# Matmuls of constants in TensorE's waits: a two-layer vision tower on one core

## The reference, cut to what matters

```
x: (32, 3, 96, 96) -> tok: 16x16 patches and four shifted copies, projected, layer norm   (32, 36, 128)
L0 attn:  norm, q/k/v, rope, softmax(q k / sqrt(16)) v over 8 heads, out; norm; W1 relu W2 (128-512-128); norm
L0 ffn:   h + gelu(norm(h) tril(W1) + b1) tril(W2) + b2
L1 attn:  two score maps, softmax(map1) - lambda * softmax(map2), times v; group norm; out_w
L1 ffn:   norm, attention (wq wk wv wo), norm, router: top 2 of 64 experts, capacity 72,
          each expert gelu(x w1 + b1) w2 + b2 (128-512-128), weighted by its gate; add
out: (32, 36, 128), float32 throughout
```

## Time and profile before

| | |
|---|---|
| three executions | 472.89, 473.05, 473.99 us; median 473.05 |
| the profiled execution | 469.0 us, of it 467.3 us span (first to last instruction) |
| mean granted clock | 0.798 |
| batches' stages | 0 to about 336 us |
| experts | about 336 to 453 us, then the sum and the stores |
| busy over the span | PE 68%, POOL 54%, DVE 48%, ACT 47% |

### The profile page before, as it was taken

How to read it: one execution, slowest core, us unless ns; L and a number is a source line. 1 busy time by engine, 2 the same in 40 slices (tenths; PEclk the granted TensorE clock), 3 DMA queues, 4 the chain that set the end, 5 groups by cost and what they waited for, 6 DMA issues and landing times.

```text
span 467.3 us, 10291 instructions
## 1 busy us (share of the span) xinstructions
PE 319.1 (68%) x3840; PEld 283.1 (61%) x3840; DVE 226.4 (48%) x642; ACT 218.2 (47%) x635; POOL 251.0 (54%) x382
## 2 busy tenths in 40 slices
PE   2867588677666675477848608325199999999970
PEld 1645557466544664365748407323199999999970
DVE  1355655853457777859474865532012222222223
ACT  0255545554678645545556614130035555555540
POOL 5176823788674334425166583788515555555560
PEclk9999669899895776765767956555569999999995
DMA  8999500000000000000000000000398998998606
GB/s 269 417 409 218 73 1 1 1 1 1 1 2 1 2 1 2 1 1 1 1 2 1 4 24 1 14 4 10 65 188 295 308 314 313 326 321 304 219 11 152
DMA packets 25818, 50.07 MB, mean 107 GB/s; under 512 B 4100, under 2 KB 16012, under 8 KB 25642
## 3 DMA queue, kind: packets, MB, share of 16 engines
q1 hardware_dynamic: 22730, 46.91, 32.4%
q0 software_dynamic: 3040, 2.52, 1.8%
HBM read 43.92 MB, written 7.72 MB: 111 GB/s over the span
## 4 chain that ended last, share of the span: by engine, by line
PE 29%; POOL 12%; DVE 6%; issue 5%; ACT 3%; DMA 2%; POOLq 0%; SPq 0%; DVEq 0%
PE bank L695 15%; PE scores L695 11%; POOL slot_rows L630 3%; PE bank L754 2%; ACT work L967 1%; POOL xrow L621 1%; POOL gn_s L672 1%; PE bank L917 1%; POOL rstd L551 1%; DVE mx L1192 1%; DMA work<-slot_rows 1%; DMA ring<-expert_rows 1%; ACT norm L967 1%; DVE work L1198 1%; POOL mid L617 1%
## 5 line engine op out<-in xcount | busy, mean ns | idle before, releaser
L695 PE MATMUL bank<-ring,work 128*72 128x128 f32 x512 | 98.2, 276 | 0.0
L967 ACT ACTIVATE work<-scores,b1T 128x72 f32<-128x72 f32 x256 | 61.4, 322 | 77.6 <-PE scores L695 77.6
L687 POOL DMA_INDIRECT expert_rows<-work,put_u x64 | 60.0, 937 | 60.3 <-issue 40.2
L695 PE MATMUL scores<-work,ring 128*128 128x72 f32 x512 | 91.7, 264 | 0.0
L695 PEld LDWEIGHTS scores<-work,ring 128*128 128x128 f32 x512 | 79.7, 198 | 0.0
L1359 DVE TENSOR_SCALAR work<-bank,work 72x128 f32<-72x128 f32 x64 | 22.2, 347 | 77.9 <-PE bank L695 77.9
L967 ACT ACTIVATE work<-bank 128x288 f32<-128x288 f32 (+3 forms) x136 | 46.4, 373 | 23.8 <-PE bank L695 12.0
L695 PEld LDWEIGHTS bank<-ring,work 128*72 128x72 f32 x512 | 54.4, 146 | 0.2 <-ACT work L967 0.2
L754 PE MATMUL bank<-cst,work 100*128 100x100 f32 x192 | 28.7, 326 | 22.0 <-POOL work L662 21.9
L662 POOL TENSOR_TENSOR work<-work,sm 100x288 f32<-100x288 f32 x32 | 26.4, 846 | 31.3 <-DVE sm L1214 25.4
L754 PEld LDWEIGHTS bank<-cst,work 100*128 100x128 f32 x192 | 26.6, 195 | 23.1 <-POOL work L662 22.6
(11 more groups left out here) (153 smaller groups left out, 619.6 us busy)
## 6 DMA issues: line engine op xcount, KB each, us to landing
ring<-in_experts SPq DMA_DIRECT2D x64, 512.0 KB, 5.1
work<-in_patches SPq DMA_DIRECT2D x4, 864.0 KB, 11.2
slot_rows<-blank SPq DMA_DIRECT2D x1, 2340.0 KB, 30.4
work<-slot_rows SPq DMA_DIRECT2D x7, 292.5 KB
wT<-in_weights SPq DMA_DIRECT2D x1, 1664.0 KB, 17.1
expert_rows<-mid POOLq DMA_DIRECT2D x2, 576.0 KB, 10.2
ring<-expert_rows SPq DMA_DIRECT2D x4, 288.0 KB, 4.7
expert_rows<-work,put_u POOLq DMA_INDIRECT x64, 4.5
```

What stands on the lines that cost most here:

```text
L687: pool.indirect_dma_start(out=ytok[:, :], out_offset=bass.IndirectOffsetOnAxis(ap=put_u[:, e:e + 1], axis=0), in_=ys[0:CAP, e % NY, :], in ...
L695: return nc.tensor.matmul(o, a, b, start=start, stop=stop)
L967: return nc.scalar.activation(o, i, f, **kw)
```

## The change

PE gets extra float32 matmuls that compute nothing of use: the 128x128 identity times 224 columns of the constants, written to the bank that the next stage is about to overwrite. A table, HOLD, says before which of PE's stages they stand and how many (125 in 34 places), and 12 more (HOLD_ROWS) stand before `x_turn(0)`, in bank 2. Each group starts with `fill` of the next stage's first job, so it waits for that bank; the wait for the stage's data comes behind the group, on the real instruction.

The rest of the diff lets each engine have its own list; `plan(engine)` returns the same list for all four, so the rows of DVE, ACT, POOL and SP are the same as before. The counts are now taken from the engine that raises them. Two semaphores are split (`rope_q_ready` from `q_ready`, `mixed` from `probs_ready`), and `values` waits for `x_turned`, which the stage before it had waited for.

```diff
+HOLD_COLS = 224
+HOLD_ROWS = 12
+HOLD = {(w.split(":")[0], int(w.split(":")[1])): int(w.split(":")[2]) for w in """
+    tok_z:0:12 src_turn:2:4 rope_flip:0:12 src_turn:3:9 rope_out:0:2 rope_flip:2:1 net_out:0:4 net_in:1:1
+    rope_pv:3:2 rope_out:3:2 mix_turn:0:3 dif_turn:0:1 dif_qk:0:1 mix_turn:2:3 dif_turn:1:3 mix_in:2:3 mix_out:3:6
+    dif_pv:0:3 gn_sum:0:2 gn_var:0:5 dif_out:0:5 dif_pv:1:6 gn_sum:1:2 dif_out:1:5 dif_pv:2:1 moe_turn:1:5
+    gn_sum:2:3 dif_out:2:2 gn_sum:3:1 moe_flip:0:11 gn_var:3:2 dif_out:3:1 moe_qk:2:1 moe_qk:3:1
+""".split()}
...
+def plan(engine):
 
     return [tuple((w.split(":")[0], int(w.split(":")[1]))) for w in ORDER_FOUND.split()]
...
             def values(stage, b, w):
+                part = {"rope_v": "src", "dif_v": "dif", "moe_v": "moe"}[stage]
+                pe.wait_ge(S["x_turned"], turned_count[part, b])
...
+            def hold(stage, b):
+
+                if HOLD.get((stage, b)):
+                    if stage in SOFT:
...
+                    else:
+                        o = fill(pe, (stage, b, 0))[:, 0:HOLD_COLS]
+                    for _ in range(HOLD[stage, b]):
+                        mm(o, const("ident"), cst[:, 0:HOLD_COLS])
...
-            for stage, b in ORDER:
+            for stage, b in ORDER["pe"]:
                 def ctx_tile(k, i):
                     return ctxT[:, TB * b + TP * i:TB * b + TP * i + TP]
 
+                hold(stage, b)
...
             bias(2, banks[0])
+            for _ in range(HOLD_ROWS):
+                mm(banks[2][:, 0:HOLD_COLS], const("ident"), cst[:, 0:HOLD_COLS])
             x_turn(0)
             x_turn(1)
```

More of the change, by code:

```diff
@@ L231, in build, with counts, by_part @@
     out_count_stages = ("rope_out", "net_out", "mix_out", "dif_out", "moe_out")
[L233 to L238, removed]
-        return found
[L241 to L248, removed]
+    def counts(engine, steps):
+        found, total = {}, 0
+        for stage, b in ORDER[engine]:
+            if stage in steps:
+                total += steps[stage]
+                found[stage, b] = total
+        return found
+    def by_part(engine, names):
+        return {(s.split("_")[0], b): n for (s, b), n in counts(engine, dict.fromkeys(names, 1)).items()}
+    norm_a = [p + "_norm_a" for p in normed_parts]
+    normed_count = by_part("act", [p + "_norm_b" for p in normed_parts])
+    turned_count = by_part("act", [p + "_turn" for p in turned_parts])
+    rstd_count = by_part("pool", norm_a)
+    var_of = counts("dve", dict.fromkeys(norm_a, 1))
+    out_count = counts("dve", dict.fromkeys(out_count_stages, 1))
+    base_count = counts("pool", {"mix_base": 1, "dif_base": 1})
+    square_n = counts("act", {"gn_center": 1, "gn_apply": 1})
+    gn_n = counts("dve", {"gn_sum": 1, "gn_var": 1})
+    k_count = counts("act", {"rope_qk": 2, "dif_qk": 4, "moe_qk": 2})
+    q_count = counts("act", {"dif_qk": 2, "moe_qk": 1})
+    v_count = counts("act", {"rope_v": 4, "dif_v": 4, "moe_v": 4})
+    hid_count = counts("act", {"net_in": FC, "mix_in": 1})
+    ctx_count = counts("act", {"rope_pv": 1, "dif_pv": 1, "moe_pv": 1})
+    probs_count = counts("pool", {"rope_sums": 1, "moe_sums": 1})
     ctx = ExitStack()
@@ L559, in rsqrt @@
                 pool.tensor_tensor(r2, r2, minus_half[0:TP, 0:TPB], ALU.pow).then_inc(S["rstd_ready"], 1)
-            sums_n = flips = 0
-            for stage, b in ORDER:
+            for stage, b in ORDER["pool"]:
                 name = stage.split("_")[0]
@@ L1134, in of @@
                 return lambda i: t[:, TPB * b + i, :]
-            soft_n = 0
-            sums_n = 0
-            flip_of = list(range(NB)) + [NB + b for b in range(NB) for _ in range(2)] + list(range(2 * NB, 3 * NB))
-            for stage, b in ORDER:
+            softs = list(soft_n)
+            for stage, b in ORDER["dve"]:
                 tok = slice(TB * b, TB * b + TB)
```

176 lines of the change are left out of this document (90 added, 86 removed).

## The result

The changed kernel takes 478.23 us, median of 20 runs (472.88 to 481.59), against 472.99 us of the kernel before (469.07 to 474.07, 20 runs beside it): ratio 1.0086, 95% interval 1.0060 to 1.0111. By the medians it is 5.2 us slower; five of the 20 runs, 480.40 us and more, count as slow and are left out of the ratio, and the other fifteen have the median 476.80 us, so that the ratio stands for 4.1 us. The predicted 475.0 us has the right sign and lies 3.2 us too low (1.8 by the fifteen); the range of 467.5 to 480 holds the time. The profiled execution took 479.02 us with a span of 477.3, the one of before 469.0 with 467.3. So the two traces lie 10.0 us apart where the medians lie 5.2 apart. The trace of before is a favourable one: 469.0 us is under all 20 runs beside the changed kernel.

What follows compares the result with a forecast made beforehand. Before 268 us a chain of four engines with none full, from 347 us experts bound by PE at full clock. Terms (a) to (i) sum to +2.0 us, carried to the median 473.05: 475.0 us, range 467.5 to 480.

Steps and rivals of the forecast that it cites:

- (a): tok_z:0: twelve matmuls in front end 2.0 us late, its full clock gives back 1.8; +0.2 us, ends -1.8 and +2.6.
- (b): src_turn:3: nine matmuls behind a bank wait are all delay, less gains at full clock behind; +2.4 us.
- (c): net_out:0: four matmuls behind a bank wait, on the path ACT waits for; +1.1 us, between -0.2 and +3.1.
- (d): net_in:1, rope_pv:3, rope_out:3: five matmuls together delay net_out:1; +0.9 us, ends +0.4 and +2.0.
- (e): Dif, mix and moe_v:0 stages: filled data waits keep the clock up and shorten stages; -3.4 us, 0 if not.
- (i): Split semaphores, the repeated wait in values and unlisted groups, said to lie in data waits; 0.
- (f): dif_pv:1: six matmuls behind a bank wait, offset by slack and faster stages behind; 0, ends -1.0 and +2.6 us.
- (g): gn_var:3's two matmuls, +0.4 us left, and moe_qk:2's one behind a bank wait, +0.4; together +0.8.
- (h): Twelve before x_turn(0): end before the rows land, clock low again by the experts; 0, or -4.5 us were it high.
- Rival 2: Groups run at the low clock and overrun even data waits, clearly slower; +8.4 us, 481.5 us, chance 0.14.
- Rival 1: Clock stays high nearly throughout, faster; -3.0 us, 470.0, or 465.5 with the experts' gain; chance 0.30.
- Rival 3: It evens out: other engines' waits absorb delays and gains alike; 473 us, chance 0.12.

Runs made afterwards that it cites:

- e1: Changed kernel with HOLD empty and HOLD_ROWS 0, leaving only split semaphores and reordered waits; 472.50 us, ratio 0.9994 to the kernel before.
- e12: Changed kernel with only the 25 data-wait groups and dif_pv:1's six in its own bank, HOLD_ROWS 0; 467.94 us, ratio 0.9946 to the kernel before.
- e11: Changed kernel with only the 25 data-wait groups and moe_qk:2's one matmul in its own bank, HOLD_ROWS 0; 466.88 us, ratio 0.9915 to the kernel before.
- e4: Changed kernel with its nine bank-wait groups writing into unused columns of scores' first bank; 470.47 us, ratio 0.9946 to the kernel before.

## Why the prediction was right, and where it was off

The mechanism was the one forecast: a group behind a bank wait is delay, a group in a data wait is a gain, and the delays weigh more. The size of the sum owes something to luck. Its bank groups came to about +5.2 us and its data groups to -3.2; the runs with each half alone have +10.1 and -5.7 (9.1 and 6.5 by the ratios). Both halves were about half of what they are, and their errors cancel in the +2.0. The step that adds the trace's +2.0 to the median is weak as well: it takes one favourable execution for the pattern of all (tok_z:1 above).

Sizes by term, from the lateness of PE's stages in the changed kernel's trace against before's, 8.4 us in all when the rows land:

- (a) +0.2 said. The twelve lasted 7.64 us (7.0 taken) and tok_z:0 3.07: it ended at 14.56 against 13.86, +0.7. Against e1's trace the changed kernel is 1.5 us early behind tok_z:1.
- (b) +2.4 said, between +1.1 and +4.8. The nine took 6.19 us, close to all low (7.0), and rope_qk:2 gave back 1.97 (4.10 to 2.13). PE was 0.7 late before and 4.5 after: +3.8, and the single-group run has +3.8 by the medians. This term is mis-sized by 1.4. The sentence that failed is "nine matmuls in a stream may raise the clock on their way": the granted clock over them was 0.58, and rose in time only for what came behind.
- (c) +1.1 said, +1.3 in the trace; (d) +0.9 said, +1.0.
- (e) -3.4 said. By the end of the mix stages the lateness had fallen from 7.4 to 5.6, by 1.7; moe_v:0 gave 0.9 as said. The place of (e)'s largest part was wrong: dif_flip:0 took 2.53 us in the changed kernel, hardly less than 2.87; a wait of 2.41 us for hid was left in front of mix_out:3 behind its six. In no profile with the data groups did it take less than 2.29, and e1 without any group has 2.20. But the run with these groups alone gained 5.7 us over its runs of before, more than the trace of one execution shows. So the data groups together, with (a) and those taken at nothing in (i), gain more than said; tok_z:1 is one place of it, the others stay open.
- (f) 0 said, end +2.6. The trace has +1.8 (5.4 to 7.1 late): the six, all at low, made dif_pv:1 5.0 us later, where 4.7 was the upper end; 1.8 of it was slack before gn_sum:1 (about 1 said), and 1.5 came back up to the end of dif_v:3 (2 said). DVE waited 3.22 us for ACT at gn_sum:1's place, where before it went on without a wait.
- (g) +0.8 said. gn_var:3 starts 0.7 later, which is gone at PE's next stage; moe_qk:2 has +2.4, since the clock had fallen there. In the trace (f) and moe_qk:2 are larger misses than (b); by the medians of e12 and e11 neither is settled.
- (h) 0 said, and 0.4 measured by itself. The bound of -4.5 us for a clock that stays high was right in size: 5.0 us (4.2 by the ratios) came when the silence was really filled. I weighed it as a lucky case of the change; it was the change's largest chance, missed by ten matmuls and four.
- (i) Split semaphores: nothing, as said (e1). But two of the groups that the prediction doesn't list, rope_out:0's two and gn_sum:2's three, stand behind a bank wait and not in a data wait; no run sizes them by themselves.
- Rival 2 falls (data groups alone are faster). Rival 1's time came for the 25 groups by themselves (0.9863 of 473.05 is 466.6 us, under its 470.0), and with the longer HOLD_ROWS it went below its 465.5, though the clock did not stay high nearly throughout (0.86 from 135 to 250 us). Rival 3 does not hold for src_turn:3 by the medians.

On the rule against it: the Trainium skill, "TensorE: Matmul & The Clock Gate", Part 4 (PE-mode transpose), says that the full clock doesn't engage for transposes, which don't count as PE being busy in the same way. The flips at full clock (1.59 us) again speak against its first half. On its second half the traces are divided. In e4 four matmuls 1.45 us behind a flip ran at the low level, six matmuls 0.61 us behind real ones at full. But in the kernel before, this flip

```profile
97.21 1.54 PE L754 MATMUL bank<-cst,work 100*128 100x100 f32 x16
```

was followed by 1.60 us of wait and then by a stage at full clock (2.18 us at 100.34). So no run here shows what transposes do to the clock later. By that rule the prediction noted +4.8 for (b) where the sum used +2.4; the trace has +3.8, between the two.

## What to carry to other kernels

Before work is put into a wait, ask what ends the wait. If the release of a buffer ends it, a filler that writes to that buffer starts only when the wait is over, and costs its whole length less what a higher clock gives back behind it. Moving it to another buffer helps only as far as it then ends in time. Then fill the wait whose following work is long and bound by the engine: 26 matmuls before the experts brought 3.9 us, while nine in front of one batch stage cost 3.8. A filler that ends some microseconds early buys nothing there, so fill up to the last short gap.

## What the runs showed of the hardware that was not expected

Two short waits were enough to bring the low level into work that keeps PE full. With nothing in the long wait for the rows, the first 15 us of the experts ran at clock 0.60. With the 22 in it and the two short waits behind them (1.07 and 1.32 us) left open, the 15 us from 332 us on had 0.66; with the 4 in the second as well, 0.89 and 1.00 in two profiled executions.

The times of the changed kernel spread more than those of before: 472.9 to 481.6 us in 20 runs against 469.1 to 474.1, and 471.0 to 476.1 in another 20. Without any extra matmul the spread is 471.3 to 474.9 in 12 runs, with bank groups alone 478.4 to 483.5 in 6, with data groups alone 464.7 to 468.6 in 5. What widens it in the changed kernel stays open. The Trainium skill, "TensorE: Matmul & The Clock Gate", Part 1 (The HAM clock gate), calls the number of slow matmuls at a start run-variable. The runs here fit that: two programs with nothing before tok_z:1 ran it at 3.07 us in one profile (before) and at 4.71 in another (e1), and the kernel with moe_qk:2's one matmul took 471.4 us in the execution in whose trace the clock had fallen there, and 466.3 in its fastest. So a trace of one execution sizes such a term only roughly: of the three single groups run by themselves, medians confirmed one (src_turn:3), not moe_qk:2, and left dif_pv:1 between two values.
